# Stores of two dense stages moved from SyncE's queue to ScalarE's, and loops written out in the last two stages

## The chip, the core and the metric

The kernel runs on one core of a Trainium2 chip. The metric is the time of one execution in microseconds, as the device reports it. Work is issued by five engines that run in order, each through its own list: TensorE (PE), VectorE (DVE), ScalarE (ACT), GpSimd (POOL) and SyncE (SP). They meet only at semaphores. SP computes nothing here: it waits and issues DMAs. DMAs that SP issues go to the hardware queue that the profile calls q1, those of ACT to q10, and GpSimd's indirect ones to q0. All three are served by the same 16 DMA engines of the core.

## The reference

A table of 50,000 nodes with 128 features passes through two graph layers. Of the edges (12,500, sorted by target) only those rows matter that are the target of one.

```python
h = jnp.maximum(_layernorm(x, axis=-1), 0.0)
x = x + _L0_gnn_ref(h, edge_index, edge_weight1, ...)   # 2 rounds of: attention over edges, skip gate, batch norm, relu, residual
h = jnp.maximum(_layernorm(x, axis=-1), 0.0)
x = x + _L1_gnn_ref(h, edge_index, edge_attr_128, ...)  # message MLP over edges, mean per target, then
#   relu(concat(x, agg, u) @ W2a + b2a) @ W2b + b2b
return x
```

`_batchnorm` takes mean and variance over all 50,000 nodes, so everything behind it needs a complete pass over the table. For a node without edges, attention and mean are zero, and the layers are dense; such rows are computed as if no node had edges, and rows with edges are computed once more and put in their place.

## The kernel before

The program is a chain of phases with a barrier of all engines between them: `prepare`, `first_layer_in`, `attention` 0, batch norm parameters, `dense_second`, `attention` 1, batch norm parameters, `dense_last`, `edge_last`. A chunk is 500 nodes (4 tiles of 125), so the dense stages have 100 chunks and 25 chunks of edge targets beside them, one for every four. Tables live in HBM, either with features down the partitions (`yT`, `hT`: 128 x 50,000) or with rows (`h2`, `x1`, `x`, `out`).

Every engine's list in a stage is made from small functions with a lag each, by one of two helpers: `unrolled` writes the list out, turn by turn; `pipeline` writes the beginning and the end out and puts a hardware loop (`Fori`) of `unroll` turns in the middle, in which addresses and semaphore targets are computed in registers. At turn t, a function with lag d works on chunk t - d, and within a turn the functions stand in the order of the list. `made(k)` is the semaphore value that says that chunk k has been made; `hold` (L115) is a wait and a semaphore increment.

`dense_second` (L687 to L891) already uses `unrolled` everywhere. SP works in pairs of chunks: `load` (L732) brings `yin` and `hin`, `load_edges` (L748) what the edge chunk needs, `store_rows` (L738) writes the pair's rows in two DMAs (112 and 13 partitions), `store_edges` (L753) and `store_y` (L744) the rest. `load` waits until the pair four before has been used; `load_edges` waits for the edge chunk two before to be finished altogether (`e.ywstats`). ACT, at turn t, does `make_sig` of chunk t - 3, `bn` of chunk t, `make_rows` of chunk t - 3 (a copy from PSUM into the buffer `rows`), then, every fourth turn, `edges_bn` or `edges_sig`. The buffer `rows` holds four chunks, that is two pairs. So `make_rows` of the first chunk of a pair waits for the landing of the store of the pair two before:

```python
act.wait_ge(rows_stored[k // 2 % 2], 16 * (k // 4) + 16)      # L776
act.wait_ge(rows_stored2[k // 2 % 2], 16 * (k // 4) + 16)     # L777
```

PE's `turn` (L872) has one PSUM buffer for the transposed rows and waits for ACT's copy of the chunk before. DVE's `make_y` (L830) has three pairs of `y` buffers and waits for the landing of the store three pairs before.

`dense_last` (L894 to L1115) has `pipeline` on every engine. SP: `load` (L945: `yin`, and `hin` and `xin` by rows, five DMAs for a pair), `load_edges` (L964, three DMAs), `store_x1` (L952, lag 4 pairs), `store_edges` (L970), `store_o` (L958, lag 9 pairs). The buffers `x1` and `o` hold four pairs each. ACT: `make_hid0`, `make_g`, `make_xn`, `bn`, `edges_bn`. `edge_last` (L1503) has `pipeline` on every engine too; its stores are GpSimd's indirect DMAs.

Of the kernel before, what the change touches and what calls it, by code (L numbers as in the profile page):

```python
# [26 lines left out]
TILE, TILES = 125, 4  # L27
CH = TILE * TILES
NCHUNK, ECHUNK = NODES // CH, EDGES // CH
SPLIT = 112  # L30
# [13 lines left out]
def made(k):  # L44


    return k + AHEAD + 1
# [67 lines left out]
def hold(sp, seen, sem, value):  # L115

    sp.wait_ge(sem, value)
    sp.sem_inc(seen, 1)
# [568 lines left out]
def dense_second(nc, a, w, scratch, edge):  # L687
# [3 lines left out]
    with phase(nc, "second") as ph:  # L691
# [25 lines left out]
        def edges(stage, unit=4):  # L717
# [4 lines left out]
                    stage(c, c % 2, c // 2)  # L722
            return step

        with nc.Block() as block:
            @block.sync
            def _(sp):
                ph.start(sp)
                sp.dma_start(src[:], a["src"].rearrange("(p t) -> p t", t=NCHUNK)).then_inc(src_loaded, 16)


                def load(t, q, r):  # L732
                    hold(sp, ph.seen, m.bn, made(2 * t + 1 - U))
                    sp.dma_start(pair_cols(yin, q), cols_of(scratch.yT, t * 2 * CH, 2 * CH)).then_inc(y_loaded[q], 16)
                    hold(sp, ph.seen, m.h2, made(2 * t + 1 - U))
                    sp.dma_start(pair_cols(hin, q), cols_of(scratch.hT, t * 2 * CH, 2 * CH)).then_inc(h_loaded[q], 16)

                def store_rows(t, q, r):  # L738
                    hold(sp, ph.seen, m.rows, made(2 * t + 1))
                    dst, s = pair_rows(scratch.h2, t * 2 * CH), t % 2  # L740
                    sp.dma_start(dst[0:SPLIT], pair(rows, s)[0:SPLIT]).then_inc(rows_stored[s], 16)
                    sp.dma_start(dst[SPLIT:TILE], pair(rows, s)[SPLIT:TILE]).then_inc(rows_stored2[s], 16)

                def store_y(t, q, r):  # L744
                    hold(sp, ph.seen, m.y, made(2 * t + 1))
                    sp.dma_start(cols_of(scratch.yT, t * 2 * CH, 2 * CH), pair_cols(y, t % 3)).then_inc(y_stored[t % 3], 16)

                def load_edges(c, s, r):  # L748
                    hold(sp, ph.seen, e.ywstats, made(c - 2))
                    sp.dma_start(eyw[:, s], cols_of(scratch.ywT, at(c) * CH)).then_inc(e_loaded[s], 16)  # L750
                    sp.dma_start(econt[:, s], run_row(scratch.ct, at(c) * CH + 1)).then_inc(e_loaded[s], 16)

                def store_edges(c, s, r):  # L753
                    hold(sp, ph.seen, e.rows, made(c))
                    move_rows(sp, rows_of(scratch.h2, NODES + at(c) * CH), flat(erows, s), erows_stored[s])

                unrolled(NCHUNK // 2, U // 2, [(0, load), (2, edges(load_edges, 2)), (5, store_rows), (6, edges(store_edges, 2)), (6, store_y)])
                for s in range(2):
                    sp.wait_ge(erows_stored[s], 16 + 32 * len(range(s, ECHUNK, 2)))
                sp.wait_ge(m.row, made(NCHUNK - 1))  # L760
                sp.dma_start(scratch.src_row.rearrange("(p t) -> p t", t=NCHUNK), src_row[:]).then_inc(src_stored, 16)
                sp.wait_ge(src_stored, 16)
                for sems in (rows_stored, rows_stored2, y_stored):
                    for q in range(len(sems)):
                        sp.wait_ge(sems[q], 16 + 16 * len(range(q, NCHUNK // 2, len(sems))))

            @block.scalar
            def _(act):
                def bn(k, q, r):
                    act.wait_ge(y_loaded[q // 2], 16 * r + 16)  # L770
                    act.wait_ge(m.h2, made(k - 2))
                    act.activation(act1[:, q % 2], yin[:, q], ACT.Relu, bias=w.bn[:, 1:2], scale=w.bn[:, 0:1]).then_inc(m.bn, 1)

                def make_rows(k, q, r):
                    act.wait_ge(m.turned, made(k))
                    act.wait_ge(rows_stored[k // 2 % 2], 16 * (k // 4) + 16)  # L776
                    act.wait_ge(rows_stored2[k // 2 % 2], 16 * (k // 4) + 16)  # L777
                    act.copy(flat(rows, k % 4), psR[0:TILE]).then_inc(m.rows, 1)

                def make_sig(k, q, r):  # L780
                    act.wait_ge(m.xz, made(k))
                    act.wait_ge(m.y, made(k - 2))
                    act.activation(sig[:, q % 2], psZ[q % 2][:, 0:CH], ACT.Sigmoid, bias=w.gate_b[:, 1:2]).then_inc(m.sig, 1)

                def edges_bn(c, s, r):
                    act.wait_ge(e_loaded[s], 32 * r + 32)
                    act.wait_ge(e.yb, made(c))
                    act.wait_ge(e.hn, made(c - 1))
                    act.activation(eact[:], eyb[:, s], ACT.Relu, bias=w.bn[:, 1:2], scale=w.bn[:, 0:1]).then_inc(e.bn, 1)
                    act.activation(eyw[:, s], eyw[:, s], ACT.Relu, bias=w.bn[:, 1:2], scale=w.bn[:, 0:1]).then_inc(e.bnw, 1)  # L790

                def edges_sig(c, s, r):
                    act.wait_ge(e.turned, made(c))
                    act.wait_ge(erows_stored[s], 32 * r + 16)
                    act.copy(flat(erows, s), psE[0:TILE]).then_inc(e.rows, 1)
                    act.wait_ge(e.xz, made(c))
                    act.wait_ge(e.yw2, made(c - 1))
                    act.activation(esig[:], psZe[:, 0:CH], ACT.Sigmoid, bias=w.gate_b[:, 1:2]).then_inc(e.sig, 1)

                unrolled(NCHUNK, U, [(3, make_sig), (0, bn), (3, make_rows), (3, edges(edges_bn)), (6, edges(edges_sig))])  # L800

            @block.gpsimd
            def _(pool):
# [90 lines left out]
def dense_last(nc, a, w, scratch, out):  # L894
# [5 lines left out]
    with phase(nc, "last") as ph:  # L900
# [31 lines left out]
        def edges(stage, unit=4):  # L932
# [3 lines left out]
                    stage(2 * r + q // unit, q // unit, r)  # L936
            return step

        with nc.Block() as block:
            @block.sync  # L940
            def _(sp):
# [7 lines left out]
                    move_rows(sp, pair(hin, q), pair_rows(scratch.h2, t * 2 * CH), x_loaded[q])  # L949
                    move_rows(sp, pair(xin, q), pair_rows(a["x"], t * 2 * CH), x_loaded[q])  # L950

                def store_x1(t, q, r):  # L952
                    hold(sp, ph.seen, m.x1, made(2 * t + 1))
                    dst = pair_rows(scratch.x1, t * 2 * CH)
                    sp.dma_start(dst[0:SPLIT], pair(x1, q)[0:SPLIT]).then_inc(x1_stored[q], 16)
                    sp.dma_start(dst[SPLIT:TILE], pair(x1, q)[SPLIT:TILE]).then_inc(x1_stored2[q], 16)

                def store_o(t, q, r):  # L958
                    hold(sp, ph.seen, m.o, made(2 * t + 1))
                    dst = pair_rows(out, t * 2 * CH)  # L960
                    sp.dma_start(dst[0:SPLIT], pair(o, q)[0:SPLIT]).then_inc(o_stored[q], 16)
                    sp.dma_start(dst[SPLIT:TILE], pair(o, q)[SPLIT:TILE]).then_inc(o_stored2[q], 16)

                def load_edges(c, s, r):  # L964
                    hold(sp, ph.seen, e.rows, made(c - 2))
                    sp.dma_start(eyn[:, s], cols_of(scratch.ydT, e_col(c))).then_inc(e_loaded[s], 16)
# [4 lines left out]
                    hold(sp, ph.seen, e.rows, made(c))  # L971
                    move_rows(sp, rows_of(scratch.x1, NODES + (ECHUNK - 1) * CH - c * CH), flat(erows, s), e_stored[s])

                pipeline(sp, NCHUNK // 2, U // 2, [(0, load), (2, edges(load_edges, 2)), (4, store_x1), (6, edges(store_edges, 2)), (9, store_o)])
                for s in range(2):
                    sp.wait_ge(e_stored[s], 16 + 32 * len(range(s, ECHUNK, 2)))
                for q in range(U // 2):
# [4 lines left out]
            def _(act):  # L982
# [22 lines left out]
                    act.wait_ge(e.h3, made(c - 2))  # L1005
                    act.activation(eact[:, s], eyn[:, s], ACT.Relu, bias=w.bn[:, 1:2], scale=w.bn_neg[:]).then_inc(e.bn, 1)

                pipeline(act, NCHUNK, U, [(9, make_hid0), (7, make_g), (5, make_xn), (0, bn), (3, edges(edges_bn))])

            @block.gpsimd  # L1010
            def _(pool):
# [14 lines left out]
                    pool.wait_ge(m.o, made(k - 8))  # L1026
                    pool.tensor_tensor(x1b[:, q], x1[:, q], w.b2b[:].rearrange("p (o f) -> p o f", o=1).to_broadcast([TILE, TILES, D]), ALU.add).then_inc(m.x1b, 1)  # L1027

                pipeline(pool, NCHUNK, U, [(0, add_h2), (3, make_rstd), (5, add_bias)])

            @block.vector
            def _(dve):
# [42 lines left out]
                    dve.wait_ge(e_stored[s], 32 * r + 16)  # L1075
                    dve.tensor_tensor(flat(erows, s), psE[0:TILE], flat(exd, s), ALU.add).then_inc(e.rows, 1)

                pipeline(dve, NCHUNK, U, [(4, edges(edges_h3)), (6, edges(edges_rows)), (9, make_hid1), (4, bias), (2, make_x1), (11, make_o), (2, stats), (2, aggr)])

            @block.tensor  # L1080
            def _(pe):
# [30 lines left out]
                    pe.wait_ge(e.rows, made(c - 1))  # L1112
                    to_rows(pe, psE, eh3[:, s], w.ident, True, e.turned)

                pipeline(pe, NCHUNK, U, [(5, edges(turn_edges)), (1, turn), (8, hidden), (6, turn_back), (10, output)])  # L1115

def by_edge(t):

# [384 lines left out]
def edge_last(nc, a, w, scratch, out):  # L1503
# [3 lines left out]
    with phase(nc, "elast") as ph:  # L1507
# [27 lines left out]
        with nc.Block() as block:  # L1535
            @block.sync
            def _(sp):
# [20 lines left out]
                        hold(sp, ph.seen, placed[q], per * r)  # L1558
                    sp.dma_start(ends[:, q], index_slot(scratch.end_index, k * CH)).then_inc(ends_loaded[q], 16)

                pipeline(sp, ECHUNK, U, [(0, load), (1, load_attr), (2, load_run), (5, load_ends)], peel=U)

            @block.gpsimd
            def _(pool):
# [10 lines left out]
                pipeline(pool, ECHUNK, U, [(0, fetch), (7, place)], peel=U)  # L1575
                for q in range(U):
                    pool.wait_ge(placed[q], per * len(range(q, ECHUNK, U)))

# [1 line left out]
            def _(dve):  # L1580
# [53 lines left out]
                pipeline(dve, ECHUNK, U, [(2, bias), (0, stats), (0, aggr), (6, output), (3, add_bias), (4, total), (5, half2), (3, half)], peel=U)  # L1634

            @block.tensor
            def _(pe):
# [50 lines left out]
                pipeline(pe, ECHUNK, U, [(3, turn), (6, output), (4, message), (3, turn_attr), (5, hidden2), (3, hidden)])  # L1688

            @block.scalar  # L1690
            def _(act):
# [36 lines left out]
                pipeline(act, ECHUNK, U, [(3, make_g), (2, make_xn), (4, make_msg), (3, make_eT), (5, half2), (3, half), (1, deviation)])  # L1728


def program(nc, a, out):
# [67 lines left out]
```

## Time and profile before

| | us |
|---|---|
| median of 3 runs | 2507.21 (2505.88 to 2508.14) |
| the profiled execution, its own time | 2495.53 |
| its span, first to last instruction | 2493.8 |
| `dense_second`, first `bn` to last statistic | 801.5 to 1191.9 |
| `dense_last`, first `bn` to last output | 1554.0 to 2090.7 |
| `edge_last`, from the first load of indices | from 2098.24 |

Busy share of the span: PE 81%, DVE 69%, ACT 55%, POOL 52%. Queue q1 (SP's DMAs) moved 441.09 MB and its packets took 56.8% of the 16 DMA engines' span; q10 (ACT's) moved 0.13 MB. A stage has to be read by itself: in `dense_second` and `dense_last` the line of the DMA engines shows nines, in `edge_last` threes and fours. A busy share of DMA near 1 says that an engine always has a packet in work, not that it moves bytes at its best rate.

### The profile page before, as it was taken

The page shows a single profiled execution, that of the slowest core. Times are in us where ns is not written, and L with a number is a line of the kernel's source. Part 1 is how long each engine was busy: PE and PEld are TensorE (multiplying, and loading weights), DVE is VectorE, ACT ScalarE, POOL GpSimd, SP SyncE. Part 2 cuts the span into 40 slices and gives each one's busy share as a digit, 9 for nine tenths or more (in the row PEclk, how much of TensorE's full clock was granted, in tenths as well). Part 3 has the DMA queues.
Part 4 walks back from the last instruction along what each step waited for, and adds up shares of the span by engine and source line. Part 5 has one row for each costly group of instructions (what it writes and reads, how often), then busy time and mean ns, then how long its engine had stood idle before and what let it go on. Part 6 is the DMA issues. An engine that isn't in the chain of part 4 may idle for free. (4 is left out here: it accounts for less than half of the span.)

```text
span 2493.8 us, 36400 instructions
## 1 busy us (share of the span) xinstructions
PE 2007.8 (81%) x7514; PEld 1147.9 (46%) x7514; DVE 1731.4 (69%) x5028; ACT 1374.2 (55%) x2609; POOL 1290.2 (52%) x1119
## 2 busy tenths in 40 slices
PE   0888888889795877787466795599989995799997
PEld 0444444444232444444233232477767774466665
DVE  3899999967896887787233896577777773455452
ACT  0988888862221666666122121467766772655652
POOL 4645554418830333333586000677777773577773
PEclk9999999999897999999787897699999997899998
DMA  4777777744122999998443232999999993344440
GB/s 142 214 225 225 234 231 225 223 148 100 31 49 84 310 320 315 317 321 291 128 123 97 65 91 85 264 294 305 300 306 309 308 283 114 95 111 103 117 107 20
DMA packets 287668, 475.76 MB, mean 191 GB/s; under 512 B 83987, under 2 KB 160672, under 8 KB 287399
## 3 DMA queue, kind: packets, MB, share of 16 engines
q1 hardware_dynamic: 237300, 441.09, 56.8%
q0 software_dynamic: 46400, 33.03, 6.5%
q8 instruction: 40, 0.66, 0.1%
q14 instruction: 104, 0.85, 0.1%
q10 hardware_dynamic: 3824, 0.13, 0.1%
HBM read 272.11 MB, written 202.60 MB: 190 GB/s over the span
## 5 line engine op out<-in xcount | busy, mean ns | idle before, releaser
L489 POOL DMA_INDIRECT first_x<-in_x,first_index x200 | 255.1, 1276 | 225.1 <-ACT first_xn L348 136.6
L348 ACT ACTIVATE first_xn<-first_x,first_nb,first_rstd 125x128 f32<-125x128 f32 x600 | 245.7, 487 | 63.5 <-issue 58.1
L808 POOL DMA_INDIRECT second_entry<-node_map,second_si x100 | 128.3, 1283 | 257.0 <-DVE second_src_row L821 218.0
L1097 PE MATMUL last_psH<-last_g,W2a 128*128 128x500 f32 x400 | 194.6, 611 | 34.7 <-DVE last_hid L1059 34.7
L1106 PE MATMUL last_psO<-W2b,last_hid 128*125 128x128 f32 x1600 | 192.0, 273 | 0.0
L1130 POOL DMA_INDIRECT elast_x<-x_rows,elast_si x100 | 140.3, 1403 | 95.7 <-issue 93.4
L879 PE MATMUL second_psZ<-second_h,gate_h 128*128 128x500 f32 x200 | 107.8, 621 | 95.5 <-DVE second_y L834 67.9
L1106 PEld LDWEIGHTS last_psO<-W2b,last_hid 128*125 128x125 f32 x1600 | 183.9, 189 | 0.9 <-issue 0.9
L348 ACT ACTIVATE last_xn<-last_x,last_nb,last_rstd 125x128 f32<-125x128 f32 x400 | 163.9, 487 | 0.1
L592 PE MATMUL first_psW<-first_h,W_in 128*128 128x500 f32 x300 | 156.6, 605 | 0.0
L1138 POOL DMA_INDIRECT out<-elast_o,elast_ends x100 | 121.6, 1216 | 62.6 <-issue 62.6
L329 DVE BATCH_NORM_STATS2 first_st<-first_x 125x6 f32<-125x128 f32 x600 | 129.6, 278 | 30.5 <-DMA first_x<-in_x 17.4
L1130 POOL DMA_INDIRECT att_rows<-h_rows,att_idx x100 | 129.2, 1292 | 35.9 <-issue 33.8
L1138 POOL DMA_INDIRECT node_map<-att_er,att_idx x100 | 128.1, 1281 | 34.2 <-issue 33.9
L1015 POOL TENSOR_TENSOR last_xh<-last_xin,last_hin 125x512 f32<-125x512 f32 x100 | 131.1, 1311 | 27.5 <-DMA last_xin<-in_x 27.2
L600 PE MATMUL first_psZ<-first_h,gate_h 128*128 128x500 f32 x200 | 103.6, 599 | 47.4 <-issue 36.5
L1371 DVE SCALAR_TENSOR_TENSOR att_dx<-att_run_cont,We_col,att_bank 128x500 f32<-128x500 f32 x50 | 36.6, 733 | 147.4 <-PE att_bank L1274 134.1
L684 POOL TENSOR_TENSOR bn_rs<-bn_rs,power 128x1 f32<-128x1 f32 x2 | 1.2, 582 | 261.2 <-DVE bn_rs L674 261.2
L355 PEld LDWEIGHTS first_psT<-ident,first_xn 125*128 125x128 f32 x600 | 76.6, 145 | 128.0 <-issue 63.8
L355 PE MATMUL first_psT<-ident,first_xn 125*128 125x125 f32 x600 | 93.3, 279 | 48.4 <-ACT first_xn L348 48.3
L329 DVE BATCH_NORM_STATS2 elast_st<-elast_x 125x6 f32<-125x128 f32 x200 | 41.1, 279 | 126.1 <-DMA elast_x<-x_rows,elast_si 126.1
L1027 POOL TENSOR_TENSOR last_x1b<-last_x,b2b 125x512 f32<-125x512 f32 x100 | 127.4, 1275 | 0.0
(266 smaller groups left out, 5276.3 us busy)
## 6 DMA issues: line engine op xcount, KB each, us to landing
hT<-first_h SPq DMA_DIRECT2D x100, 250.0 KB
yT<-first_y SPq DMA_DIRECT2D x100, 250.0 KB, 2.2
second_yin<-yT SPq DMA_DIRECT2D x50, 500.0 KB
second_hin<-hT SPq DMA_DIRECT2D x50, 500.0 KB
yT<-second_y SPq DMA_DIRECT2D x50, 500.0 KB
last_yin<-yT SPq DMA_DIRECT2D x50, 500.0 KB
first_x<-in_x SPq DMA_DIRECT2D x100, 224.0 KB
h_rows<-second_rows SPq DMA_DIRECT2D x50, 448.0 KB
```

Of the source, the lines that this page charges most:

```text
L329: last = dve.bn_stats(st[:, j], x[:, j])
L348: last = act.activation(xn[:, j], x[:, j], ACT.Relu, bias=nb[:, j:j + 1], scale=rstd[:, j:j + 1])
L355: last = pe.transpose(ps[:, j * TILE:(j + 1) * TILE], rows[:, j], ident[0:TILE, 0:TILE])
L489: pool.indirect_dma_start(x[:, to % X, j], None, a["x"], bass.IndirectOffsetOnAxis(index[:, end, r % 2, j:j + 1], 0), bounds_check=NODES - ...
L592: pe.matmul(psW[k % 2][:, 0:CH], w.W_in[:], h0[:, k % 2], start=True, stop=True).then_inc(m.w_in, 1)
L808: pool.indirect_dma_start(entry[:, q], None, scratch.node_map, bass.IndirectOffsetOnAxis(si[:, q], 0), bounds_check=NODES - 1, oob_is_err= ...
L1015: pool.tensor_tensor(xh[:, q % 4], xin[:, q], hin[:, q], ALU.add).then_inc(m.xh, 1)
L1027: pool.tensor_tensor(x1b[:, q], x1[:, q], w.b2b[:].rearrange("p (o f) -> p o f", o=1).to_broadcast([TILE, TILES, D]), ALU.add).then_inc(m. ...
L1097: last = pe.matmul(psH[h][:, 0:CH], w.W2a[:, 0, h * 128:(h + 1) * 128], g[:, q % 2], start=True, stop=True)
L1106: last = pe.matmul(psO[q % 2][0:TILE, j * D:(j + 1) * D], tile_cols(hid[:, q % 4, h], j, False), w.W2b[:, h], start=(h == 0), stop=(h == 1))
L1130: pool.indirect_dma_start(rows[:, j], None, table, bass.IndirectOffsetOnAxis(index[:, j:j + 1], 0), bounds_check=table.shape[0] - 1, oob_i ...
L1138: pool.indirect_dma_start(table, bass.IndirectOffsetOnAxis(index[:, j:j + 1], 0), rows[:, j], None, bounds_check=table.shape[0] - 1, oob_i ...
```

## The change

In `dense_second` the functions `store_rows` and `store_y` leave SP's list and are put, with the same waits and DMAs, at the end of ACT's list; in `dense_last` the same is done with `store_x1` and `store_o`. ACT's turns are chunks and not pairs, so a helper `pairs` calls the store on odd chunks only. All lists of `dense_last` and `edge_last` but the ones already written out go from `pipeline` to `unrolled`. No buffer, no size and no computed value is changed.

```diff
+        def pairs(stage):
+            def step(k, q, r):
+                if k % 2 == 1:
+                    stage(k // 2, k // 2 % (U // 2), k // 2 // (U // 2))
+            return step
...
 # dense_second, SP
-                unrolled(NCHUNK // 2, U // 2, [(0, load), (2, edges(load_edges, 2)), (5, store_rows), (6, edges(store_edges, 2)), (6, store_y)])
+                unrolled(NCHUNK // 2, U // 2, [(0, load), (2, edges(load_edges, 2)), (6, edges(store_edges, 2))])
 # dense_second, ACT
-                unrolled(NCHUNK, U, [(3, make_sig), (0, bn), (3, make_rows), (3, edges(edges_bn)), (6, edges(edges_sig))])
+                def store_rows(t, q, r):
+                    hold(act, ph.seen, m.rows, made(2 * t + 1))
+                    dst, s = pair_rows(scratch.h2, t * 2 * CH), t % 2
+                    act.dma_start(dst[0:SPLIT], pair(rows, s)[0:SPLIT]).then_inc(rows_stored[s], 16)
+                    act.dma_start(dst[SPLIT:TILE], pair(rows, s)[SPLIT:TILE]).then_inc(rows_stored2[s], 16)
+                def store_y(t, q, r):
+                    hold(act, ph.seen, m.y, made(2 * t + 1))
+                    act.dma_start(cols_of(scratch.yT, t * 2 * CH, 2 * CH), pair_cols(y, t % 3)).then_inc(y_stored[t % 3], 16)
+                unrolled(NCHUNK, U, [(3, make_sig), (0, bn), (3, make_rows), (3, edges(edges_bn)), (6, edges(edges_sig)),
+                                     (5, pairs(store_rows)), (6, pairs(store_y))])
 # dense_last, SP
-                pipeline(sp, NCHUNK // 2, U // 2, [(0, load), (2, edges(load_edges, 2)), (4, store_x1), (6, edges(store_edges, 2)), (9, store_o)])
+                unrolled(NCHUNK // 2, U // 2, [(0, load), (2, edges(load_edges, 2)), (6, edges(store_edges, 2))])
 # dense_last, ACT (store_x1 and store_o as they were, with act in place of sp)
-                pipeline(act, NCHUNK, U, [(9, make_hid0), (7, make_g), (5, make_xn), (0, bn), (3, edges(edges_bn))])
+                unrolled(NCHUNK, U, [(9, make_hid0), (7, make_g), (5, make_xn), (0, bn), (3, edges(edges_bn)), (5, pairs(store_x1)), (13, pairs(store_o))])
 # dense_last: POOL, DVE, PE; edge_last: SP, POOL, DVE, PE, ACT
-                pipeline(pool, NCHUNK, U, [(0, add_h2), (3, make_rstd), (5, add_bias)])
+                unrolled(NCHUNK, U, [(0, add_h2), (3, make_rstd), (5, add_bias)])
...
```

## Rows read from the trace of the kernel before

**Rows 1.** Stretch; busy PE, PEld, DVE, ACT, POOL; granted clock; DMA share; GB/s.

```profile
900.00:950.00 50.00, 39.31 (x129) 20.77 (x130) 40.93 (x87) 33.84 (x55) 16.50 (x14) 1.00 0.98 329
...
1750.00:1800.00 50.00, 44.72 (x290) 35.56 (x289) 36.09 (x122) 35.76 (x73) 36.40 (x39) 1.00 1.02 302
...
2200.00:2300.00 100.00, 100.00 (x366) 65.99 (x365) 50.34 (x171) 62.15 (x117) 76.87 (x59) 1.00 0.44 112
```

**Rows 2.** Who waited for whom in 900:1100: us in total, times, longest.

```profile
DVE second_y L834 <- DMA yT<-second_y: 38.8, 14, 4.0
...
ACT second_rows L778 <- DMA h_rows<-second_rows: 27.9, 25, 1.9
...
ACT second_esig L798 <- PE second_psXe L889: 11.8, 13, 1.1
```

**Rows 3.** DMA issues in 900:1100, and the queue of TensorE's instructions.

```profile
q8 instruction: 5, 0.08, 0.2%
...
second_yin<-yT SPq DMA_DIRECT2D x26, 500.0 KB
```

**Rows 4.** ACT in order of time in 953.5:972: start, us, idle before and releaser.

```profile
956.23 0.57 ACT L778 COPY second_rows<-second_psR 125x512 f32<-125x512 f32 x1
956.69 0.59 ACT L795 COPY second_erows<-second_psE 125x512 f32<-125x512 f32 x1
958.23 0.68 ACT L798 ACTIVATE second_esig<-second_psZe,gate_b 128x500 f32<-128x500 f32 x1 [0.94 <-PE second_psXe L889]
...
962.25 0.57 ACT L778 COPY second_rows<-second_psR 125x512 f32<-125x512 f32 x1
962.71 0.81 ACT L789 ACTIVATE second_eact<-second_eyb,bn 128x500 f32<-128x500 f32 x1
963.42 0.80 ACT L790 ACTIVATE second_eyw<-second_eyw,bn 128x500 f32<-128x500 f32 x1
964.12 0.66 ACT L783 ACTIVATE second_sig<-second_psZ,gate_b 128x500 f32<-128x500 f32 x1
964.68 0.80 ACT L772 ACTIVATE second_act<-second_yin,bn 128x500 f32<-128x500 f32 x1
965.37 0.58 ACT L778 COPY second_rows<-second_psR 125x512 f32<-125x512 f32 x1
...
970.96 0.59 ACT L778 COPY second_rows<-second_psR 125x512 f32<-125x512 f32 x1 [1.52 <-DMA h_rows<-second_rows]
```

**Rows 5.** SP in order of time: one store in the stage, one at its end.

```profile
966.27 0.42 SPq L742 DMA_DIRECT2D h_rows<-second_rows  x1
...
1189.09 0.42 SPq L149 DMA_DIRECT2D h_rows<-second_erows  x1
...
1191.80 0.28 SPq L761 DMA_DIRECT2D src_row<-second_src_row  x1
```

**Rows 6.** SP's waits over the second stage (800:1192).

```profile
SPq L118 <- DVE wends L862: 105.9, 23, 6.8
```

**Rows 7.** Issues by tile: ns least/median/most, first and last start.

```profile
L746 SPq DMA_DIRECT2D yT<-second_y x50: 350/528/1502, 830.1 to 1190.1; - x50
...
L955 SPq DMA_DIRECT2D x_rows<-last_x x50: 317/346/4528, 1574.4 to 2059.4; - x50
L956 SPq DMA_DIRECT2D x_rows<-last_x x50: 434/948/1990, 1578.8 to 2059.8; - x50
...
L961 SPq DMA_DIRECT2D out<-last_o x50: 317/330/1417, 1627.9 to 2091.4; - x50
L962 SPq DMA_DIRECT2D out<-last_o x50: 318/433/1588, 1628.7 to 2091.8; - x50
```

**Rows 8.** Groups of ACT in 1650:2050: busy, mean ns, idle before, releaser.

```profile
L1006 ACT ACTIVATE last_eact<-last_eyn,bn,bn_neg 128x500 f32<-128x500 f32 x20 | 16.1, 804 | 40.4 <-DMA last_exd<-xd_rows 40.3
```

**Rows 9.** SP's issue of that load, and the instruction it held up.

```profile
1697.22 1.45 SPq L968 DMA_DIRECT2D last_exd<-xd_rows  x1
...
1711.89 0.81 ACT L1006 ACTIVATE last_eact<-last_eyn,bn,bn_neg 128x500 f32<-128x500 f32 x1 [3.22 <-DMA last_exd<-xd_rows]
```

More of the change, by code:

```diff
@@ L736, in load @@
                     sp.dma_start(pair_cols(hin, q), cols_of(scratch.hT, t * 2 * CH, 2 * CH)).then_inc(h_loaded[q], 16)
[L738 to L746, printed above, removed]
                 def load_edges(c, s, r):
@@ L937, in edges, with pairs, step @@
             return step
+        def pairs(stage):
+            def step(k, q, r):
+                if k % 2 == 1:
+                    stage(k // 2, k // 2 % (U // 2), k // 2 // (U // 2))
+            return step
         with nc.Block() as block:
@@ L950, in load @@
                     move_rows(sp, pair(xin, q), pair_rows(a["x"], t * 2 * CH), x_loaded[q])
[L952 to L962, printed above, removed]
                 def load_edges(c, s, r):
@@ L1006, in edges_bn, with store_x1, store_o @@
                     act.activation(eact[:, s], eyn[:, s], ACT.Relu, bias=w.bn[:, 1:2], scale=w.bn_neg[:]).then_inc(e.bn, 1)
-                pipeline(act, NCHUNK, U, [(9, make_hid0), (7, make_g), (5, make_xn), (0, bn), (3, edges(edges_bn))])
+                def store_x1(t, q, r):
+                    hold(act, ph.seen, m.x1, made(2 * t + 1))
+                    dst = pair_rows(scratch.x1, t * 2 * CH)
+                    act.dma_start(dst[0:SPLIT], pair(x1, q)[0:SPLIT]).then_inc(x1_stored[q], 16)
+                    act.dma_start(dst[SPLIT:TILE], pair(x1, q)[SPLIT:TILE]).then_inc(x1_stored2[q], 16)
+                def store_o(t, q, r):
+                    hold(act, ph.seen, m.o, made(2 * t + 1))
+                    dst = pair_rows(out, t * 2 * CH)
+                    act.dma_start(dst[0:SPLIT], pair(o, q)[0:SPLIT]).then_inc(o_stored[q], 16)
+                    act.dma_start(dst[SPLIT:TILE], pair(o, q)[SPLIT:TILE]).then_inc(o_stored2[q], 16)
+                unrolled(NCHUNK, U, [(9, make_hid0), (7, make_g), (5, make_xn), (0, bn), (3, edges(edges_bn)), (5, pairs(store_x1)), (13, pairs(store_o))])
             @block.gpsimd
@@ L1076, in edges_rows @@
                     dve.tensor_tensor(flat(erows, s), psE[0:TILE], flat(exd, s), ALU.add).then_inc(e.rows, 1)
-                pipeline(dve, NCHUNK, U, [(4, edges(edges_h3)), (6, edges(edges_rows)), (9, make_hid1), (4, bias), (2, make_x1), (11, make_o), (2, stats), (2, aggr)])
+                unrolled(NCHUNK, U, [(4, edges(edges_h3)), (6, edges(edges_rows)), (9, make_hid1), (4, bias), (2, make_x1), (11, make_o), (2, stats), (2, aggr)])
             @block.tensor
@@ L1113, in turn_edges @@
                     to_rows(pe, psE, eh3[:, s], w.ident, True, e.turned)
-                pipeline(pe, NCHUNK, U, [(5, edges(turn_edges)), (1, turn), (8, hidden), (6, turn_back), (10, output)])
+                unrolled(NCHUNK, U, [(5, edges(turn_edges)), (1, turn), (8, hidden), (6, turn_back), (10, output)])
 def by_edge(t):
@@ L1559, in load_ends @@
                     sp.dma_start(ends[:, q], index_slot(scratch.end_index, k * CH)).then_inc(ends_loaded[q], 16)
-                pipeline(sp, ECHUNK, U, [(0, load), (1, load_attr), (2, load_run), (5, load_ends)], peel=U)
+                unrolled(ECHUNK, U, [(0, load), (1, load_attr), (2, load_run), (5, load_ends)])
             @block.gpsimd
@@ L1573, in place @@
                     scatter_ends(pool, ph.seen, out, o[:, q], ends[:, q], placed[q])
-                pipeline(pool, ECHUNK, U, [(0, fetch), (7, place)], peel=U)
+                unrolled(ECHUNK, U, [(0, fetch), (7, place)])
                 for q in range(U):
@@ L1632, in output @@
                     dve.tensor_tensor(flat(o, q), psO[0:TILE], flat(xb, q), ALU.add).then_inc(m.o, 1)
-                pipeline(dve, ECHUNK, U, [(2, bias), (0, stats), (0, aggr), (6, output), (3, add_bias), (4, total), (5, half2), (3, half)], peel=U)
+                unrolled(ECHUNK, U, [(2, bias), (0, stats), (0, aggr), (6, output), (3, add_bias), (4, total), (5, half2), (3, half)])
             @block.tensor
@@ L1686, in hidden2 @@
                     last.then_inc(m.hidden2, 1)
-                pipeline(pe, ECHUNK, U, [(3, turn), (6, output), (4, message), (3, turn_attr), (5, hidden2), (3, hidden)])
+                unrolled(ECHUNK, U, [(3, turn), (6, output), (4, message), (3, turn_attr), (5, hidden2), (3, hidden)])
             @block.scalar
@@ L1726, in half2 @@
                     act.activation(hid2[:, q % 2, 0], psG[0][:, 0:CH], ACT.Relu, bias=w.b2u[:, 0:1]).then_inc(m.hid20, 1)
-                pipeline(act, ECHUNK, U, [(3, make_g), (2, make_xn), (4, make_msg), (3, make_eT), (5, half2), (3, half), (1, deviation)])
+                unrolled(ECHUNK, U, [(3, make_g), (2, make_xn), (4, make_msg), (3, make_eT), (5, half2), (3, half), (1, deviation)])
 def program(nc, a, out):
```

## The prediction

> **What bounds the kernel now.** I read the busy times by stretch first, since the averages of the page mix stages [rows 1]. In the second dense stage no compute engine is full (PE 39.3 of 50 us, DVE 40.9, ACT 33.8), while the DMA engines are at 0.98. In the last dense stage PE is at 44.7 of 50 us and DMA at 1.02. In the edge stage PE has 100.00 of 100 us at full clock and DMA 0.44: PE alone bounds it, so I expect nothing there from lists written out.
>
> A DMA share near 1 doesn't say which wait ends last, so the waits come next. In 200 us of the second stage DVE's `make_y` waited 38.8 us for landings of `y` stores, and ACT's `make_rows` 27.9 us, 25 times for 26 pairs, for landings of row stores [rows 2, 3]. The timeline shows what that is: the copy of a pair's last chunk ended at 956.80 (956.23 + 0.57) [rows 4], SP issued the second DMA of its store at 966.27 [rows 5], and the copy of the first chunk two pairs on, which needs that buffer, started at 970.96 [rows 4]. So a store is 9.5 us late at its issue and lands 4.6 us after it. The lateness is SP's order: stores stand behind `load_edges`, whose wait for the edge chunk two before cost SP 105.9 us in 23 waits [rows 6]. The second stage runs on the chain copy, store, landing, copy. Its pair takes 200 / 26 = 7.69 us [rows 3].
>
> In the last stage one pair takes 10.0 us (20 edge chunks, one per two pairs, in 400 us [rows 8]). Its visible DMA wait is the edge load: 40.4 us before `edges_bn` [rows 8]; one load was issued at 1697.22 and held ACT for 3.22 us until 1711.89, 14.6 us later [rows 9].
>
> **Part 1: second stage, row stores on ACT.** It removes the 5 to 9 us behind SP, but puts the store at lag 5 in ACT's order. Chunk 2p+1 is copied at turn 2p+4, its store is issued at the end of turn 2p+6, behind the copy of chunk 2p+3, and the copy of chunk 2p+4 in turn 2p+7 waits for its landing. Only `make_sig` and `bn` (0.56 + 0.70 us from start to start [rows 4]) stand between issue and wait. Two pairs of buffers work as one. ACT now stalls for the rest of each landing, and everything behind it (sig, bn, PE's `turn`) stalls too. From one landing to the next:
> - semaphore to start, 0.10, and copy of 2p+4, 0.46 (962.25 to 962.71) [rows 4];
> - `edges_bn`, every other pair: (0.71 + 0.70) / 2 = 0.70 [rows 4];
> - `store_y` issue, 0.35 at least [rows 7], with its wait and increment 0.45;
> - `make_sig` 0.56, `bn` 0.69, copy of 2p+5 0.58 and 0.10 to its semaphore [rows 4]: 1.93;
> - `edges_sig`, every other pair: from the end of the copy to the end of `esig`, 956.80 to 958.91, is 2.11, of which 0.94 is a wait for PE [rows 4, 2]; half is 1.05;
> - first store issue with its gap, 0.42 (both DMAs are issued like L955's least, 0.32 [rows 7], plus 0.1).
>
> Sum 5.1 us, and then the landing L, counted from the second issue. L was 4.6 us in the stage, behind loads in one queue [rows 4, 5]. At the stage's end, with no loads in flight, the last piece of an edge store issued at 1189.09 right behind other stores had landed at 1191.80 [rows 5]: 2.7. On ACT's queue no load stands ahead of the store, and the next pair's loads are released by the `bn` of turn 2p+7, after the store has been issued; the erows store of SP goes out at the same moment every other pair. I take 3.1, near the unloaded end. 5.1 + 3.1 = 8.2 us for a pair against 7.69: +0.5 over 48 pairs, **+25 us**. Ends: without PE's 0.94 (0.47 a pair) and L 2.7 it is 7.3, -16 us; with L 4.6 it is 9.7, +98 us.
>
> The `y` stores: `store_y` goes out at turn 2t+7, the buffer is wanted by DVE for chunk 2t+6 at its turn 2t+10. Three turns are 11.5 us against a landing of some 5; the 38.8 us of waits go away. They give nothing: the row chain is late next. SP keeps loads and edge traffic; its 105.9 us wait then holds up only loads, which run seven chunks ahead. POOL's lookups aren't moved past anything.
>
> The row above shows a store that lands 4.6 us after its issue behind queued loads, 2.7 without [rows 4, 5]. The Trainium skill (DMA: Bandwidth & Descriptors, Queues, rings and completion order) says that each DMA engine goes round robin over the rings that have work, packet by packet. By that rule the store would share with loads and not queue behind them; no row here has both queues at work.
>
> **Part 2: last stage, x1 and o stores on ACT.** Their buffers hold four pairs: an x1 store goes out at turn 2p+6 and is wanted at DVE's turn 2p+10, an o store at 2p+14 for 2p+19, 20 and 25 us; landings don't matter. What counts is ACT's time. It is busy 35.76 of 50 us [rows 1], 7.15 a pair, and waits 1.0 a pair for the edge load (40.4 / 40) [rows 8]. Four issues, all on even turns, take 1.39 us at their least and 2.06 at their medians [rows 7]; two holds and gaps add about 0.5. So ACT gets 10.0 to 10.7 us of a 10.0 us pair. On the other side SP sheds four of its issues, edge loads can leave earlier, and the register work of loops on ACT goes. I take +0.2 us a pair: **+10 us**. Ends: if the edge wait vanishes and PE alone is left, 44.72 / 5 = 8.9 us a pair, -1.06 over 45 pairs, -48 us; if each of the four issues takes the 0.95 of L956's median [rows 7], 7.15 + 3.8 + 0.5 = 11.4, +70 us.
>
> The stage moves 302 GB/s at a DMA share of 1.02 with SP's queue alone [rows 1]. The Trainium skill (DMA: Bandwidth & Descriptors, Issuing engines are not separate DMA queues) says that all issuing engines end on the same DMA engines and that a second issuer saves only the time to initiate. That speaks against a gain; by it the loads would come no sooner, and this stage would stay at its 10.0 us a pair at best.
>
> **Part 3: no loops.** In the edge stage PE has no idle time [rows 1], so a back edge or a register instruction removed is worth nothing; in the last stage it hides beside DMA and PE. Written-out lists have to be fetched: the second stage is one already, and fetched TensorE's five times in 200 us for 0.08 MB of its 63 [rows 3], at 0.2% of DMA. Bounds: -5 us (head and tail of two stages) to +5. I take 0.
>
> **Sum.** 2495.53 + 25 + 10 + 0 = 2530 by the profiled execution. The median of the runs before is 2507.21, 11.7 above it, so the forecast is 2507.2 + 35 = **2542 us**.
>
> **Rivals.**
> - *The last stage gains more than the second loses.* The place is the edge load: taken out from among the stores, SP issues it turns earlier and ACT's 3.2 us stall every 20 us goes; PE becomes the bound, -48. For it: PE has only 44.7 of 50 and the load lands 14.6 us after issue. Against: DMA share 1.02, and ACT's own budget. It decides when the last stage's pair falls under 9.5 us. 2507 + 25 - 48 = 2484.
> - *ACT stalls in issuing.* Issues on SP reach 4.5 us [rows 7] when the DMA engines are behind; if ACT meets the same, the last stage costs +70 and the second, with three issues lengthened by 0.3 each, +45: 2507 + 115 = 2622. Against: ACT's queue holds only a third of the bytes.
> - *The change doesn't do what it says:* both stages are held by DMA bandwidth (0.98, 1.02) and stay: 2507 ± 5.
>
> **How the numbers follow.** Forecast 0.50, edge load rival 0.26, ACT issue rival 0.14, no change 0.10. The likeliest case alone spans 2515 to 2580 (L 2.9 to 3.9). With the rivals taken in from both sides, the range is 2475 to 2610. About 0.2% (5 us) is what can be told from no change. Faster: the edge load rival and a little of the forecast's low end, 0.28. Same: 0.09. Slower: 0.63.
>
> **What would show it.** Right, if `make_rows` waits for row stores 2 to 3 us once a pair on ACT, `make_y` no longer waits for landings, and the pair of the second stage is 8.0 to 8.6 us; if in the last stage ACT is at 9 of 10 us with its issues, and the edge stage is unchanged. Wrong in part 1, if landings on ACT's queue take under 2.6 us or the wait falls elsewhere; wrong in part 2, if `edges_bn` stops waiting and the pair falls below 9.7, or if issues on ACT exceed 0.6 us each.

## The result, and the profile after

The changed kernel takes 2574.21 us (median of 4 runs, 2564.4 to 2577.86) against 2506.55 (2498.13 to 2508.14) before: ratio 1.0273, 95% interval 1.0252 to 1.0294. That is 68 us more, in the forecast's direction and inside its range, and about twice the 35 us of its sum.

By stage, from the two profiles (spans 2493.8 and 2562.6 us): the second dense stage, from its first `bn` to its last `y`, went from 385.3 to 438.3 us (+53); the last dense stage, from its first `bn` to its last output, from 536.7 to 546.7 (+10); from there to the end 403.1 and 403.6. The rest (5 us) lies between the two stages.

The busy times by stretch after answer to [rows 1]: stretch, length, busy PE, PEld, DVE, ACT, POOL, granted clock, DMA share, GB/s.

```profile
900.00:950.00 50.00, 36.43 (x111) 19.17 (x110) 35.74 (x76) 28.38 (x46) 15.27 (x12) 0.90 0.84 285
1750.00:1800.00 50.00, 43.70 (x274) 33.57 (x273) 36.67 (x117) 34.10 (x70) 35.61 (x38) 1.00 1.01 303
2300.00:2400.00 100.00, 100.00 (x363) 65.57 (x363) 53.35 (x187) 62.83 (x117) 77.21 (x59) 1.00 0.43 109
```

In the second stage every resource does less in the same time: DMA falls from 0.98 to 0.84, PE, DVE and ACT with it. A new wait has come, not a new load. The last stage moves 303 GB/s in this row (over the longer window 1650:1950, 296 after against 304 before), and in the edge stage PE is still at 100.00 of 100.

The waits in 900:1100 (us in total, times, longest) answer to [rows 2], the last line (SP's own waits over the whole stage, 800:1250) to [rows 6]:

```profile
ACT second_rows L775 <- DMA h_rows<-second_rows: 45.3, 21, 5.1
...
ACT second_esig L795 <- PE second_psXe L897: 23.1, 11, 2.7
...
DVE second_y L842 <- DMA yT<-second_y: 2.0, 1, 2.0
...
SPq L118 <- DVE wends L870: 241.0, 23, 13.2
```

`make_y` hardly waits for landings any more (2.0 us, 38.8 before), and `make_rows` waits 45.3 instead of 27.9 us. SP's wait for the edge chunk has grown from 105.9 to 241.0 us; only loads and edge traffic stand behind it now. Why `make_rows` waits is seen in ACT's order of time over two pairs (ACTq is a DMA issue); compare [rows 4]:

```profile
985.90 0.31 ACTq L800 DMA_DIRECT2D h_rows<-second_rows  x1
986.25 0.46 ACTq L801 DMA_DIRECT2D h_rows<-second_rows  x1
...
989.11 0.59 ACT L775 COPY second_rows<-second_psR 125x512 f32<-125x512 f32 x1 [0.24 <-DMA h_rows<-second_rows]
989.34 0.34 ACTq L805 DMA_DIRECT2D yT<-second_y  x1
...
990.57 0.34 ACTq L800 DMA_DIRECT2D h_rows<-second_rows  x1
990.94 1.85 ACTq L801 DMA_DIRECT2D h_rows<-second_rows  x1
990.99 0.66 ACT L780 ACTIVATE second_sig<-second_psZ,gate_b 128x500 f32<-128x500 f32 x1
991.55 0.79 ACT L769 ACTIVATE second_act<-second_yin,bn 128x500 f32<-128x500 f32 x1
...
993.47 0.79 ACT L769 ACTIVATE second_act<-second_yin,bn 128x500 f32<-128x500 f32 x1
997.48 0.58 ACT L775 COPY second_rows<-second_psR 125x512 f32<-125x512 f32 x1 [3.22 <-DMA h_rows<-second_rows]
```

and what SP issued at the same time:

```profile
988.80 0.32 SPq L747 DMA_DIRECT2D second_eyw<-ywT  x1
989.17 0.43 SPq L748 DMA_DIRECT2D second_econt<-ct  x1
989.70 0.36 SPq L148 DMA_DIRECT2D h_rows<-second_erows  x1
990.12 0.42 SPq L149 DMA_DIRECT2D h_rows<-second_erows  x1
990.65 1.86 SPq L741 DMA_DIRECT2D second_yin<-yT  x1
```

The reader is to see two landings. The store issued at 986.25 had no other transfer issued by SP or ACT in the 5 us before it and had landed when the copy began at 989.11, 2.8 us later. The one issued at 990.94 was 1.6 us behind 500 KB of `y` in its own queue and within 2.2 us of 1.25 MB on SP's; its landing released the copy at 997.48, 6.5 us later. So it goes in turn: over pairs 4 to 45 the landing after the second issue is 2.97 us in even and 7.05 in odd pairs, mean 5.0. (The landings in this document are worked out from the updates of the DMAs' semaphores in the trace.) The store's lateness (from the end of the pair's last copy to that issue) is 9.55 us in the mean, against 6.5 before. From the end of a copy to the reuse of its buffer 14.5 us pass, before 12.2 (6.5 + 5.7), and the pair has gone from 7.72 to 8.87 us.

A second thing stands in these rows: the issues of 990.57 and 990.94 come ahead of `make_sig` (990.99), `bn` (991.55) and the copy behind it in time, although ACT's list has the three before the store, and run beside ACT's computation, the second one for 1.85 us. ACT's queue of instructions runs ahead of its arithmetic. The stall that a late landing causes is real, the issue times are not added to ACT's work.

A third thing is the granted clock, 0.90 in the first row above where it was 1.00 before. During the stall TensorE has nothing to do: it waited 2.74 us for ACT's copy until 981.28, and behind that the clock stood at the lower of its two levels (1.2 GHz in place of 2.4):

```profile
981.00:985.00 4.00, 3.72 (x11) 2.71 (x12) 1.92 (x3) 2.61 (x5) 1.27 (x1) 0.57 1.02 373
```

This comes back once every two pairs, and it meets TensorE's matmuls for the edge chunk, for which ACT's `edges_sig` waits in the same chain. Their durations (ns, least, median, most) and ACT's idle time before `edges_sig` (us, times), first before, then after:

```profile
L888 PE MATMUL second_psZe<-second_eyw,gate_h x50: 582/584/585, 820.6 to 1187.7; 128*128 128x500 f32 x50
...
  PE second_psXe L889: 23.3, 25
```

```profile
L896 PE MATMUL second_psZe<-second_eyw,gate_h x50: 582/1041/1042, 819.1 to 1244.6; 128*128 128x500 f32 x50
...
  PE second_psXe L897: 51.6, 25
```

The wait for TensorE has grown from 0.93 to 2.06 us, once in two pairs: an estimate of 0.57 us a pair, about half of the 1.15 by which the pair grew. No run holds the clock fixed, so the division is an estimate. That the lower clock follows the stall is seen in e3 below: without the stall it is at 1.00 again.

In the last stage, the wait for the edge load answers to [rows 8] (1700:2100 after), the issues by tile to [rows 7]. The two lines between show all waits for that load in the same window, 1650:1950, before and after:

```profile
L1009 ACT ACTIVATE last_eact<-last_eyn,bn,bn_neg 128x500 f32<-128x500 f32 x19 | 15.3, 803 | 44.8 <-DMA last_exd<-xd_rows 44.7
```

```profile
ACT last_eact L1006 <- DMA last_exd<-xd_rows: 31.0, 14, 3.5
```

```profile
ACT last_eact L1009 <- DMA last_exd<-xd_rows: 48.8, 13, 10.9
```

```profile
L1015 ACTq DMA_DIRECT2D x_rows<-last_x x50: 454/457/732, 1638.5 to 2139.9; - x50
...
L1021 ACTq DMA_DIRECT2D out<-last_o x50: 456/535/1857, 1687.4 to 2160.2; - x50
```

SP, without its stores, does issue that load earlier: 17.0 us before ACT is free for it in the mean of edge chunks 3 to 22, against 12.5 before. But the last of the edge chunk's three loads now lands 19.2 us after that issue, against 14.3.

### The profile page after: what moved, and what is told of

It is laid out like the page before. It is cut to its first block and busy times, and to the rows that moved or that the text cites. A ratio compares the mean times of both kernels' runs of the same rounds, so it can differ in the third digit from the quotient of the medians.

```text
span 2562.6 us, 34220 instructions
## 1 busy us (share of the span) xinstructions
PE 2040.0 (80%) x7514; PEld 1162.6 (45%) x7514; DVE 1743.6 (68%) x5028; ACT 1375.3 (54%) x2609; POOL 1288.6 (50%) x1119
## 5 line engine op out<-in xcount | busy, mean ns | idle before, releaser
L361 PE MATMUL second_psR<-ident,second_h 128*125 128x128 f32 x400 | 73.5, 310 | 83.1 <-ACT second_rows L775 83.1
L361 PEld LDWEIGHTS second_psR<-ident,second_h 128*125 128x125 f32 x400 | 58.6, 203 | 154.6 <-ACT second_rows L775 140.9
```

The costliest lines, as they stand in the source:

```text
L361: last = pe.transpose(ps[0:TILE, j * D:(j + 1) * D], tile_cols(t, j, ordered), ident[:])
```

## The experiments

Each kernel was timed beside the kernel before on the same chip (ratio and 95% interval). "Pair" is the mean time of two chunks, "late" the time from the end of a pair's last copy to the second issue of its row store, "landing" from that issue to its last landing (pairs 4 to 45); the lengths of stages go from the start of the first `bn` to the start of the last `y` and of the last `o`. Lengths, pairs, lateness and landings come from one profile of each kernel.

| kernel | ratio | second, us | pair | late | landing | last, us | pair |
|---|---|---|---|---|---|---|---|
| before | 1 | 385.3 | 7.72 | 6.5 | 5.7 | 536.7 | 10.04 |
| the change | 1.0273 (1.0252 to 1.0294) | 438.3 | 8.87 | 9.6 | 5.0 | 546.7 | 10.17 |
| e1_second_only | 1.0262 (1.0236 to 1.0288) | 444.4 | 8.94 | 9.7 | 5.0 | 535.5 | 10.03 |
| e2_loops_only | 0.9987 (0.9962 to 1.0012) | 382.0 | 7.60 | 6.3 | 5.6 | 543.0 | 10.17 |
| e3_rows_lag3 | 0.9852 (0.9820 to 0.9884) | 339.3 | 6.71 | 1.1 | 6.6 | 545.0 | 10.21 |
| e5_y_lag7 | 1.0209 (1.0173 to 1.0246) | 423.0 | 8.54 | 8.7 | 5.0 | 547.2 | 10.23 |
| e7_lag3_old_last | 0.9844 (0.9819 to 0.9869) | 340.9 | 6.73 | 1.1 | 6.5 | 534.7 | 9.98 |
| e8_sp_lag4 | 1.0040 (1.0020 to 1.0060) | 390.0 | 7.78 | 0.5 | 4.8 | 539.4 | 10.12 |
| e9_last_only | 1.0036 (1.0021 to 1.0051) | 388.1 | 7.75 | 6.6 | 5.7 | 549.3 | 10.28 |
| e10_exd_split | 0.9691 (0.9667 to 0.9715) | 345.2 | 6.83 | 1.1 | 6.7 | 498.9 | 9.35 |
| e11_sp_both | 0.9869 (0.9842 to 0.9897) | 350.6 | 6.95 | 0.9 | 7.1 | 542.5 | 10.16 |
| e12_split_old_last | 0.9750 (0.9726 to 0.9774) | 343.7 | 6.81 | 1.1 | 6.6 | 513.5 | 9.62 |
| e13_before_split | 0.9899 (0.9871 to 0.9926) | 385.8 | 7.72 | 6.3 | 5.9 | 511.9 | 9.61 |

**e1_second_only: only the second stage changed.**

> Only the second dense stage changed; the last two stages as before, with loops and with stores on SP. Theory (the chain copy, late store, landing, copy in the second stage carries the loss): the stage stays at 8.9 us a pair, 54 to 58 us over before, time 2560 to 2567. Rival (a good part of the loss comes from ACT's issues or the written-out lists in the last two stages): under 2550.

Measured 2566.95 us, +2.62%: nearly all of the loss is the second stage's.

**e9_last_only: only the last two stages changed.**

> The second stage as before; the last two stages as changed (x1 and o stores on ACT, no loops). Theory (last stage 10 us longer, edge stage equal): 2512 to 2520. Rival (what looked like 10 us in single profiles is their scatter): 2505 within 5 us.

Measured 2508.90 us, +0.36% (+5 to +13 us): small, but clear of zero. With e1 it makes up the whole (0.36 + 2.62 = 2.98 against 2.73, within the intervals). The time itself is under the 2512 to 2520 expected and inside the rival's 2505 within 5; it is the ratio, against 2499.03 for the kernel before on this chip, that tells it from scatter. The edge load lands 19.2 us after its issue here too.

**e2_loops_only: loops written out, no store moved.**

```diff
-                pipeline(sp, NCHUNK // 2, U // 2, [... (4, store_x1), ... (9, store_o)])
+                unrolled(NCHUNK // 2, U // 2, [... (4, store_x1), ... (9, store_o)])
 # the same for every other list of the last two stages
```

> Only the loops of the last two stages written out; all stores on SP as before. Theory (back edges and register work are hidden, and so is the fetching of longer lists): 2507 within 5 us. Rival (fetching longer lists disturbs the last stage, and that is its 11 us): 2515 to 2520.

Measured 2504.01 us, interval of the ratio about -9.5 to +3 us: no difference that the whole time shows. Its profile has the last stage at 543.0 us. Without the split of below, the five kernels with a looped last stage have it at 534.7 to 542.5 us (middle 536.7), the four written out with stores on ACT at 545.0 to 549.3. So a share of the 10 us may belong to the written-out lists; single profiles scatter too much to say how much. The timed runs bound it: the intervals of e2 (0.9962 to 1.0012) and e9 (1.0021 to 1.0051), which differ by the moved stores alone, do not touch, so the stores cost something by themselves. The edge load goes with them: it lands after 15.1 us in e2 and 19.2 in e9. What the lists add is seen in the queues of instructions over 1650:2050 (packets, MB, share), first e2, then before:

```profile
q8 instruction: 19, 0.31, 0.4%
q14 instruction: 29, 0.24, 0.2%
```

```profile
q8 instruction: 1, 0.02, 0.0%
q14 instruction: 1, 0.01, 0.0%
```

**e3_rows_lag3: the store issued right behind its copy.**

```diff
-                                     (5, pairs(store_rows)), (6, pairs(store_y))])
+                                     (3, pairs(store_rows)), (6, pairs(store_y))])
```

> The changed kernel with store_rows of the second stage at lag 3 in place of 5, so it is issued right behind the copy of the pair's second chunk. Theory (it is the late issue): issue within 1 us of the copy's end in place of 9.5, waits of make_rows for landings under 20 us in the stage in place of 98, the stage at 7.4 to 7.8 us a pair, time 2505 to 2522. Rival (two queues at once, or ACT's issuing itself, cost the time): the pair stays over 8.5 us, time 2560 or more.

Measured 2464.53 us, -1.48%: from 68 us slower to 37 us faster (0.0148 x 2504.8) by one number. The theory stood and its size was too small (2505 to 2522 expected). Copy and issue now stand together:

```profile
899.85 0.58 ACT L775 COPY second_rows<-second_psR 125x512 f32<-125x512 f32 x1
900.52 0.31 ACTq L800 DMA_DIRECT2D h_rows<-second_rows  x1
900.87 0.79 ACTq L801 DMA_DIRECT2D h_rows<-second_rows  x1
```

and the busy times of 900:1100, in the columns of [rows 1], show what is next:

```profile
900.00:1100.00 200.00, 175.63 (x597) 96.08 (x596) 183.88 (x388) 146.10 (x239) 77.17 (x60) 1.00 1.01 366
```

Landings of rows are longer than before (6.6 us) and nobody waits for one; for `y` DVE waits 5.6 us in all. DVE is busy 184 of 200 us, and the granted clock is back at 1.00. And DMA moves 366 GB/s where the stage before had 318 at a share of 0.96 over the same window. The high share of before was no bound.

**e5_y_lag7: the `y` store no longer just ahead of the row store.**

```diff
-                                     (5, pairs(store_rows)), (6, pairs(store_y))])
+                                     (5, pairs(store_rows)), (7, pairs(store_y))])
```

> The changed kernel with store_y of the second stage at lag 7 in place of 6, so it is issued behind the row store of the same turn and not 1.6 us ahead of it. Theory (the 7.1 us landings, every second pair, come from 500 KB of y ahead in ACT's queue): these landings fall to 5 or 6 us, the pair from 8.9 to 8.3 or 8.5, time 2545 to 2560. Rival (they come from the loads on SP's queue that start at the same moment): landings stay at 7, time 2570 to 2578.

Measured 2554.30 us, +2.09%. Odd pairs' landings fell from 7.05 to 6.10 us, even ones rose from 2.97 to 3.91, for a mean of 5.0 as before, and a wait for `y` came in. The waits of 900:1100:

```profile
DVE second_y L842 <- DMA yT<-second_y: 50.9, 16, 6.9
...
ACT second_rows L775 <- DMA h_rows<-second_rows: 32.5, 19, 4.8
```

So taking the 500 KB of `y` from ahead of the row store moved about 1 us from odd to even landings. What makes odd ones longer by the 2.2 us that are left (the transfers of SP's queue that start in the same 2 us, or `y`, which now follows right behind) is not shown: no run took either away. The time of 2545 to 2560 was forecast, but not by this way: with the mean landing equal, the pair fell by 0.33 us, and what fell with it is the wait before `edges_sig`, from 2.1 to 1.25 us in the mean, 0.4 a pair. That wait is 0.91 us in the 17 edge chunks that no stretch of lower clock meets and 2.67 in the 4 that one does; in the change, one met 18 of 21.

**e8_sp_lag4 and e11_sp_both: is it the queue, or the place in the order?**

```diff
 # e8, SP's list of the second stage in the kernel before
-  [(0, load), (2, edges(load_edges, 2)), (5, store_rows), (6, edges(store_edges, 2)), (6, store_y)]
+  [(0, load), (2, edges(load_edges, 2)), (4, store_rows), (6, edges(store_edges, 2)), (6, store_y)]
 # e11
+  [(0, load), (2, edges(load_edges, 2)), (4, store_rows), (5, store_y), (6, edges(store_edges, 2))]
```

> The kernel before with one number changed: store_rows of the second stage at lag 4 pairs in place of 5, still on SP and on SP's queue. Theory (what counts is when the store is issued, not whose queue it is on): issue lateness falls from 6.5 us to 2 or 3, waits for row landings mostly go, pair 7.0 to 7.5, time 2475 to 2500. Rival (the gain at lag 3 on ACT comes from the second queue): 2505 within 5 us.

> The kernel before with both stores of the second stage one pair earlier in SP's order (rows at lag 4, y at lag 5 and ahead of the edge store), all still on SP's queue. Theory (with rows alone moved, y was late next; with both early the waits for landings go without a second queue): pair of the second stage 6.8 to 7.3 us, time 2465 to 2485. Rival (on one in-order issuer a store that leaves early holds up the loads and other stores, so only a second issuer gives the gain): 2495 to 2512.

e8: 2510.70 us against 2499.03 on its chip, +0.40%. The expected gain did not come. The row store left 0.5 us after its copy, `make_rows` stopped waiting, and the time rose a little. Waits of 900:1100 in e8:

```profile
PE second_psZ L879 <- DVE second_y L834: 46.4, 44, 2.3
DVE second_y L834 <- DMA yT<-second_y: 41.7, 15, 4.3
```

The `y` chain was as late as the row chain and took its place. e11 moved both: 2469.11 us, -1.31%, pair 6.95, with row landings of 7.1 us that nobody waits for. All stores were still on SP's queue. Against it, the same kernel with stores on ACT (e7) has -1.56%; the intervals (0.9842 to 0.9897, 0.9819 to 0.9869) overlap. What gives nearly all of the gain is that both stores leave in time. The second queue adds 6 us by the medians of the ratios, and the intervals allow from nothing to some 15. The profiles point to a small share: the second stage is 350.6 us long in e11 and 339.3 to 345.2 in the four kernels with the row store on ACT at lag 3, and in e11 DVE waits 19.0 us in 900:1100 for an edge load on SP's queue, of which e3 and e7 show nothing.

**e7_lag3_old_last: e3's second stage, last two stages as before.**

> Second stage with its stores on ACT and store_rows at lag 3; the last two stages as before (loops, stores on SP). Theory (the second stage gives 42 to 46 us when the store leaves at once; the last stage is some 10 us shorter as it was before): 2452 to 2460, below the 2464.5 of the kernel with lag 3 and the changed last stages. Rival (the last stages are worth nothing either way): 2462 to 2468.

Measured 2458.51 us, -1.56%, against -1.48% for e3: inside both intervals, so whether the last stages of before are better here is not shown by it.

**e10, e13, e12: the edge load of the last stage.**

```diff
-                    sp.dma_start(flat(exd, s), rows_of(scratch.xd, e_col(c))).then_inc(e_loaded[s], 16)
+                    move_rows(sp, flat(exd, s), rows_of(scratch.xd, e_col(c)), e_loaded[s])
...
-                    act.wait_ge(e_loaded[s], 48 * r + 48)
+                    act.wait_ge(e_loaded[s], 64 * r + 64)
```

> As the kernel with lag 3, and the edge load of xd rows in the last stage in two DMAs of 112 and 13 partitions, as all other row transfers, in place of one of 125. Theory (that load lands 14 to 19 us after its issue because its 125 partitions are spread over few DMA engines, which also carry the most work): landing falls by 4 us or more, the 53 us of ACT's waits for it shrink to under 20, the last stage by 10 to 30 us, time 2435 to 2455. Rival (it is late because the whole queue is behind, at a DMA share of 1): waits stay over 40 us, time 2460 to 2468.

> The kernel before with only the xd load of the last stage split in 112 and 13 partitions. Theory (the last stage's DMA load sat on few engines): last stage 40 to 48 us shorter, time 2452 to 2462. Rival (the split needs the changed stages around it): over 2485.

> Second stage with stores on ACT, rows at lag 3; last stage with loops and stores on SP as before, but its xd load in two DMAs of 112 and 13 partitions. Theory (the split gives its 40 us whoever issues the stores, and the old last stage is worth some 8 more): 2408 to 2418. Rival (the split pays only with the stores on ACT's queue): over 2435.

e10, on top of e3: 2422.62 us, -3.09%, the fastest kernel of this study. The last stage is 46 us shorter than e3's, where 10 to 30 were expected, and the edge load lands after 15.2 us in place of 19.2. Its stretch 1650:1950 and its wait for the load:

```profile
1650.00:1950.00 300.00, 291.00 (x1857) 228.20 (x1856) 236.88 (x801) 226.80 (x464) 241.05 (x256) 1.00 1.04 330
...
ACT last_eact L1009 <- DMA last_exd<-xd_rows: 15.0, 13, 2.3
```

PE is at 97% and DMA at 330 GB/s; in the same window it moved 304 GB/s at a share of 1.02 before and 296 at 1.00 after the change. Alone in the kernel before (e13) the split gave 2478.39 us, -1.0%, the last stage 25 us shorter and the load landing after 11.5 us in place of 14.3: less than the 40 to 48 us I expected, and faster than the rival's 2485. With the old last stage and the new second one (e12) it gave 2437.91, -2.5%; 2408 to 2418 was expected, so that expectation failed, and the time is in the rival's range. The rival's reason does not hold as it was put: against e7, which has no split, e12 is 1% faster (0.9750 against 0.9844, intervals apart), so the split pays with the stores on SP's queue too, only about half as much:

```profile
1650.00:1950.00 300.00, 284.62 (x1812) 223.02 (x1812) 230.65 (x778) 221.02 (x453) 236.73 (x250) 1.00 1.04 317
...
ACT last_eact L1014 <- DMA last_exd<-xd_rows: 22.1, 15, 2.3
POOL last_xh L1023 <- DMA last_xin<-in_x: 16.5, 21, 1.7
```

Here POOL's `add_h2` waits 16.5 us for `xin` and DMA is slower by 13 GB/s than in e10. So the stores on ACT's queue (with the lists written out) are worth 15 us (0.6%, 0.9691 against 0.9750, intervals apart) once the edge load is out of the way, and cost 9 us (e9) while it is not. Which of the two, stores or lists, gives the 15 was not tried.

## Why the prediction was right, and where its sizes were off

Direction, stage and wait came as forecast. That the time fell inside the range owes something to luck: the sum was half of what was measured, and inside it errors of opposite sign met. Of its own signs, `make_rows` waits 45.3 us in 200, 2.0 a pair, as forecast (2 to 3), though unevenly, and `make_y` has all but stopped waiting; but the pair is at 8.87 us and not at 8.0 to 8.6, and ACT's busy time in the last stage did not rise.

**The bound named was the right one.** "The second stage runs on the chain copy, store, landing, copy": e3 and e11 take the lateness out of the chain and the stage falls by 35 to 46 us. One link was missing for the kernel before: the `y` chain was just as tight, as [rows 2] had shown with 38.8 us. e8 shows it.

**Part 1, direction and place right, size too small.** Predicted +25 us, measured +53. The stall fell where the step put it, on `make_rows` once a pair. The term that was mis-sized is the landing: taken as 3.1 us "near the unloaded end", measured 5.0 in the mean, 2.97 and 7.05 in turn. (The pair that I read for the kernel before, 9.5 us late and 4.6 to land, was no mean one either: 6.5 and 5.7.) The step had put the next loads behind the store; the rows show `yin` issued 0.3 us ahead of its second part, edge loads and the edge store before that, and I had left `store_y`, moved by the same change to the same queue, out of the landing of its neighbour. The sum of ACT's own steps was off the other way: 5.1 us predicted, 8.87 - 5.0 = 3.9 measured. From the copy's start to the second issue the step has 4.7 us for pairs with `edges_bn`, and 1.8 were measured, since the issue runs ahead of arithmetic that the list has before it; for pairs with `edges_sig` it has 5.4, and 5.7 were measured, since the wait for TensorE, taken as 0.94 us as before, had grown to 2.06 with the lower clock. The clock was no term of the sum. With the landing alone put right the sum would have been 10.1 us and the forecast nearly 60 us too high.

**Part 2, size right by luck, mechanism not.** Predicted +10, measured +10 in the profile and +9 timed (e9). But it was built on ACT's time being full, and ACT is busy 34.10 of 50 us after, with less than before. Issues up to 1.9 us long on ACT did not stretch its work. What the runs show in its place is the edge load: in the kernels with their last-stage stores on ACT's queue and no split it lands after 19.0 to 19.2 us, in the other kernels without it after 14.2 to 15.1, and ACT's wait for it grew from 31.0 to 48.8 us in 300. Only lists written out (e2) give -9.5 to +3 us; how much of the 9 us is theirs is open.

**Part 3** held in the edge stage: 403.1 and 403.6 us from the last output on.

**Rivals.** That ACT stalls in issuing is not borne out by the rows above. That DMA bandwidth holds both stages is refuted: 366 and 330 GB/s were reached in the same stages. The edge load rival named the right obstacle, but its remedy fell short: with the stores out of SP's order the load is issued 4.5 us earlier and lands 4.9 us later. In 1650:1950 the wait is 31.0 us before, 48.8 after the change, 40.2 in e3, and 15.0 once the load is split (e10).

The Trainium skill (DMA: Bandwidth & Descriptors, Why a DMA increments its semaphore by 16 and not by 1) says that a DMA of hardware queues uses the largest number of DMA engines, up to 16, that divides the slowest dimension of both its sides; by it, 125 partitions go over 5 engines, 112 over 16 and 13 over 13. e10, e12 and e13 agree with it: their only edit to the load is 125 into 112 + 13, and it lands 2.5 to 4 us sooner. That the number of engines is the reason is not shown: the packets by engine are not in the trace, and two DMAs of another division of the 125 were not tried.

## What to carry to other kernels

When a transfer frees a buffer that its issuer, or the engine feeding it, will want, write down three times: end of the producer, issue, landing, and compare their sum with the buffers' depth; then look which store, of all that share the order, is late next. Moving an issue to another engine's list helps by its place there, and with a wrong lag makes two buffers act as one. A DMA share near 1 need be no bandwidth bound: 318 GB/s became 366 by a changed order, 298 (e3) became 330 (e10) by splitting one load in two. And a stall costs more than its length where it lets TensorE's clock fall: look at the granted clock, and at one matmul's duration, before and after.

## What the runs showed of the hardware that was not expected

- ACT's DMA issues run ahead of and beside its arithmetic: an issue at 990.94 of 1.85 us beside activations started at 990.99 and 991.55, which the list has before it.
- The same 500 KB row store lands 2.8 us after its second issue when nothing else was issued near it, and after 6.5 us within some 2 us of 1.75 MB of other transfers on both queues (means of even and odd pairs: 2.97 and 7.05).
- With pauses of TensorE once every two pairs the granted clock fell to its lower level nearly each time (18 of 21 edge chunks), and the same 128x500 matmul took 1041 ns in place of 584 (medians).
- One load of 250 KB in 125 partitions every 20 us, 4% of the stage's bytes, cost the kernel 25 us (e13) to 42 (e10 against e3: 2464.5 to 2422.6) against the same load in two DMAs of 112 and 13 partitions.
